# A graph layer's tensor product, built with features on partitions

## What is computed

```
def tensor_product(x_e, sh, w, C):          # C: [64, 9, 128], once for keys, once for values
    acc = sh[:, 0:1] * (x_e @ C[:, 0, :])
    for s in range(1, S):
        acc = acc + sh[:, s:s + 1] * (x_e @ C[:, s, :])
    return acc * w
```

## Time and profile before

| | |
|---|---|
| median of the runs | 3732.7 us |
| the profiled execution's own time | 3729.88 us |
| its span, first to last instruction | 3728.2 us |
| granted TensorE clock, mean | 0.942 |
| TensorE / VectorE / ScalarE / GpSimd busy | 89% / 77% / 34% / 55% |
| first edge loop, stage between, second edge loop | 170 to 1242, to 1406, to 3592 us |

### The profile page before, as it was taken

One profiled execution on the slowest core, in us unless ns is written; L12 is line 12 of the kernel. 1 busy time (PEld: TensorE's weight loads), 2 busy tenths in 40 slices (PEclk: granted clock), 3 DMA queues, 4 the chain that ended last, 5 costly groups with the idle time before them and its releaser, 6 DMA issues. The chain is left out here.

```text
span 3728.2 us, 86642 instructions
## 1 busy us (share of the span) xinstructions
PE 3330.0 (89%) x25947; PEld 3178.9 (85%) x25947; DVE 2877.5 (77%) x5292; ACT 1285.0 (34%) x3333; POOL 2055.4 (55%) x1999
## 2 busy tenths in 40 slices
PE   2099999999999337999999999999999999999963
PEld 1088888888888237999999999999999999999953
DVE  4366666666666227999999999999999999999943
ACT  1033333333333113444444444444444444444420
POOL 2577777777777435555555555555555555555540
PEclk9599999999999658999999999999999999999975
DMA  8399999999999313444444444444444444444420
GB/s 339 86 268 280 279 279 279 279 280 279 279 280 279 105 46 105 127 126 132 131 124 129 131 129 124 130 132 126 125 132 132 124 128 131 130 124 129 132 78 29
DMA packets 843789, 622.16 MB, mean 167 GB/s; under 512 B 490431, under 2 KB 732803, under 8 KB 843452
## 3 DMA queue, kind: packets, MB, share of 16 engines
q1 hardware_dynamic: 667110, 500.09, 44.2%
q0 software_dynamic: 56640, 87.65, 9.7%
q10 hardware_dynamic: 119982, 33.79, 4.1%
HBM read 335.87 MB, written 286.31 MB: 167 GB/s over the span
## 5 line engine op out<-in xcount | busy, mean ns | idle before, releaser
L1305 POOL DMA_INDIRECT xg<-h_tab,src_i x808 | 861.5, 1066 | 220.8 <-issue 127.2
L789 POOL DMA_INDIRECT kv<-kv_tab,src_i x808 | 762.1, 943 | 285.7 <-issue 188.2
L1315 POOL TENSOR_TENSOR kq<-kvs,q_of 128x512 f32<-128x512 f32 x202 | 260.6, 1290 | 837.7 <-DVE kvs L1491 837.7
L1401 ACT ACTIVATE z_hi<-bank 128x512 fp32r<-128x512 f32 x808 | 439.4, 595 | 802.9 <-PE bank L1333 802.9
L1357 PE MATMUL bank<-C_hi,z_hi 128*128 128x256 f32 x4040 | 682.2, 299 | 0.0
L1357 PE MATMUL bank<-C_lo,z_hi 128*128 128x256 f32 x4040 | 612.2, 281 | 0.0
L1481 DVE TENSOR_TENSOR z_lo<-bank,z_hi 128x512 fp32r<-128x512 f32 x808 | 520.5, 686 | 113.5 <-ACT z_hi L1401 113.4
L1357 PEld LDWEIGHTS bank<-C_hi,z_hi 128*128 128x128 f32 x4040 | 537.8, 191 | 0.3
L1357 PEld LDWEIGHTS bank<-C_lo,z_hi 128*128 128x128 f32 x4040 | 535.3, 188 | 0.0
L1357 PE MATMUL bank<-C_hi,z_lo 128*128 128x256 f32 x3232 | 516.2, 281 | 0.0
L913 DVE TENSOR_TENSOR wsb<-bank,b 128x512 f32<-128x512 f32 x404 | 279.3, 691 | 298.7 <-PE bank L977 298.3
(11 more groups left out here) (248 smaller groups left out, 4754.4 us busy)
## 6 DMA issues: line engine op xcount, KB each, us to landing
w_tab<-wsb SPq DMA_DIRECT2D x202, 512.0 KB, 3.4
win<-w_tab SPq DMA_DIRECT2D x202, 512.0 KB, 3.6
sum_edge<-rowt SPq DMA_DIRECT2D x202, 288.0 KB, 2.5
q_edge<-zq SPq DMA_DIRECT2D x202, 256.0 KB
qs<-q_edge SPq DMA_DIRECT2D x202, 256.0 KB, 2.8
sum_edge<-rows ACTq DMA_DIRECT2D x202, 136.0 KB
qs<-q_edge SPq DMA_DIRECT2D x202, 128.0 KB
drow<-dst_tab SPq DMA_DIRECT2D x202, 128.0 KB, 3.2
```

The source lines that it names most:

```text
L789: pool.indirect_dma_start(kv[b][:, q, :], None, kv0_tab, bass.IndirectOffsetOnAxis(ap=src_i[:, i * Q + q:i * Q + q + 1], axis=0))\
L1305: pool.indirect_dma_start(xg[b][:, q, :], None, h1_tab, bass.IndirectOffsetOnAxis(ap=src_i[:, i * Q + q:i * Q + q + 1], axis=0))\
L1315: pool.tensor_tensor(kq[:, :].rearrange("p (q o) -> p q o", q=Q), kvs[b][:, :, 0:O1], q_of[b % 2][:, :].rearrange("p (q o) -> p q o", q=Q) ...
L1401: nc.scalar.activation(z_hi[b % 2][:, k, :], bank[ZB[k]][:, :], ACT.Copy).then_inc(hi_out, 1)
```

## The change

z is no longer built with edges on partitions and turned. The node rows are turned instead (two transposes), ScalarE writes the turned rows `xT` twice (features on both halves of the partitions), and VectorE multiplies `xT` with spherical numbers that are already the same on all 64 partitions of a half. Of the four pairs of such rows, two are loaded repeated from DRAM (`sh`), and two are spread by TensorE into PSUM from a high and a low part (`sh_split`, eight rows, with a selection matrix `pick`); the ninth number is loaded repeated too (`sh_last`). z then lies in SBUF, and the high and low parts are formed from there, 1024 columns at a time. The comparison for `same1` goes from VectorE to ScalarE as four squares and one relu. For all this the spherical numbers must lie turned in DRAM: the stage between the loops gets a part that loads them, 101 passes at a time on 101 (or 100) partitions, rearranges them and stores three tables. The core of the diff:

```
+            SG = NST // 2
+            sh_rows = [sb(f"sh_rows{g}", [SG, ST, S], F32, ph) for g in range(2)]
+            sh_parts = sb("sh_parts", [SG, 5, ST], F32, ph)
+            sh_split = sb("sh_split", [SG, 8, ST], F32R, ph)
...
+                    def load_sh_rows(a):
+                        last_full = (NST - 1) * ST
+                        sp.dma_start(sh_rows[0][:, :, :], a[0:SG * ST, :].rearrange("(p e) s -> p e s", p=SG))\
+                          .then_inc(sh_rows_in, 16)
+                        sp.dma_start(sh_rows[1][0:NST - 1 - SG, :, :],
+                                     a[SG * ST:last_full, :].rearrange("(p e) s -> p e s", e=ST)).then_inc(sh_rows_in, 16)
+                        sp.dma_start(sh_rows[1][NST - 1 - SG:NST - SG, 0:TAIL, :], a[last_full:E, :].unsqueeze(0))\
+                          .then_inc(sh_rows_in, 16)
...
                     sp.dma_start(car[:, :, :], carry0_tab[0:N, :].rearrange("(p j) d -> p j d", j=NJ)).then_inc(car_got, 16)
+                    for g in range(2):
+                        sp.wait_ge(sh_parts_set, g + 1)
+                        sp.dma_start(sh_tab[g * SG:(g + 1) * SG], sh_parts[:, 0:4, :]).then_inc(sh_put, 16)
+                        sp.dma_start(sh_last_tab[g * SG:(g + 1) * SG, :], sh_parts[:, 4, :]).then_inc(sh_put, 16)
+                        sp.wait_ge(sh_split_set, g + 1)
+                        sp.dma_start(sh_split_tab[g * SG:(g + 1) * SG], sh_split[:, :, :].bitcast(F32)).then_inc(sh_put, 16)
                     sp.wait_ge(h1_ready, 1)
...
+                    act.wait_ge(sh_rows_in, 48)
+                    for g in range(2):
+                        if g:
+                            act.wait_ge(sh_put, 48)
+                        nc.scalar.activation(sh_split[:, 0:4, :], sh_rows[g][:, :, 4:S - 1].rearrange("p e c -> p c e"), ACT.Copy)\
+                                 .then_inc(sh_split_hi, 1)
...
+                        ins.then_inc(sh_parts_set, 1)
...
                     dve.sem_inc(shift_ready, 1)
+                    for g in range(2):
+                        dve.wait_ge(sh_split_hi, g + 1)
+                        dve.tensor_tensor(sh_split[:, 4:8, :], sh_rows[g][:, :, 4:S - 1].rearrange("p e c -> p c e"),
+                                          sh_split[:, 0:4, :].bitcast(F32), ALU.subtract).then_inc(sh_split_set, 1)
                     dve.wait_ge(own_got, 16 * NJ)
...
-                    pipelined(sp, [(load_sh, 3), (load_drow, 2), (load_q, 2), (load_mask, 1), (store, -4), (load_w, 1)], RING)
+                    pipelined(sp, [(load_split, 4), (load_sh_last, 4), (load_sh, 3), (load_drow, 2), (load_q, 2), (load_mask, 1), (store, -4), (load_w, 1)], RING)
...
-                    unrolled([(times_q, -1), (gather_x, 4)], RING)
+                    unrolled([(times_q, -1), (gather_x, 5)], RING)
...
-                    pipelined(pe, [(t_z(0), 1), (t_z(1), 1), (turn_max, -2), (sums, -3), (m_acc(0), 0), (t_z(2), 1),
-                                   (t_z(3), 1), (m_acc(1), 0), (t_z(4), 1), (spread_q, 0), (m_acc(2), 0),
-                                   (turn_logits, -1), (m_acc(3), 0)], RING)
+                    pipelined(pe, [(turn_x, 3), (turn_max, -2), (sums, -3), (m_acc(0), 0), (spread_q, 0), (m_acc(1), 0),
+                                   (turn_logits, -1), (m_acc(2), 0), (m_acc(3), 0), (spread_sh, 3)], RING)
...
-                    pipelined(act, [(hi(0), 1), (hi(1), 1), (copy_max, -2), (weights, -2), (take_sums, -3), (hi(2), 1),
-                                    (hi(3), 1), (hi(4), 1), (take_q, 0)], RING)
+                    pipelined(act, [(hi(0), 1), (copy_max, -2), (weights, -2), (take_x, 3), (take_sums, -3), (take_q, 0),
+                                    (hi(1), 1), (hi_last, 1), (apart, 1), (build, 1)], RING)
...
-                    pipelined(dve, [(product(1), -1), (lo(0), 1), (lo(1), 1), (subtract, -2), (outer(0), 2), (lo(2), 1),
-                                    (lo(3), 1), (logits, -1), (weigh, -2), (outer(1), 2), (lo(4), 1), (build, 1),
-                                    (segment_max, -1), (product(0), 0)], RING)
+                    pipelined(dve, [(product(1), -1), (subtract, -2), (outer_spread, 2), (logits, -1), (weigh, -2), (lo(0), 1),
+                                    (outer, 2), (lo(1), 1), (lo_last, 1), (outer_last, 3), (segment_max, -1),
+                                    (product(0), 0)], RING)
```

More of the change, by code:

```diff
@@ new lines, in apart @@
+                    def apart(it, i, b):
+                        act.wait_ge(drow_in[b % 2], 16 * (2 * it + b // 2 + 1))
+                        need(act, sum_mm, i - RING + 1)
+                        for q in range(Q):
+                            ins = nc.scalar.activation(same[b][:, q, :], drow[b % 2][:, q * P:(q + 1) * P], ACT.Square,
+                                                       bias=dst_e[:, bass.ds(i * Q + q, 1)], scale=-1.0)
+                        ins.then_inc(apart_ready, 1)
@@ L1409, in take_q, with build @@
+                    def build(it, i, b):
+                        act.wait_ge(apart_ready, i + 1)
+                        nc.scalar.activation(same[b][:, :, :], same[b][:, :, :], ACT.Relu, bias=one[:, :], scale=-1.0)\
+                                 .then_inc(same_ready, 1)
+                    act.wait_ge(max_zero, 4)
                     def take_q(it, i, b):
@@ new lines, in _ @@
+                    dve.memset(one[:, :], 1.0).then_inc(max_zero, 1)
+                    for c in range(2):
+                        dve.tensor_tensor(pick[c][:, :].rearrange("p (r i) -> p r i", r=2),
+                                          bcast(ident[0:8, 2 * c:2 * c + 2], 2, D), bcast(ident[0:8, 2 * c + 4:2 * c + 6], 2, D),
+                                          ALU.add).then_inc(max_zero, 1)
+                    dve.memset(seg_max[:, :], 0.0).then_inc(max_zero, 1)
+                    dve.wait_ge(max_zero, 4)
@@ new lines, in outer, with outer_spread @@
+                    def outer(it, i, b):
+                        dve.wait_ge(x_out, i + 1)
+                        dve.wait_ge(sh_in[b % 2], 32 * (2 * it + b // 2 + 1))
+                        need(dve, lo_out, i * 3 - 4)
+                        dve.tensor_tensor(z[b % 2][:, 0:2, :], bcast(xT[b % 2][:, :], 1, 2), sh[b % 2][:, :, :], ALU.mult)\
+                           .then_inc(z_ready, 1)
+                    def outer_spread(it, i, b):
+                        dve.wait_ge(x_out, i + 1)
+                        dve.wait_ge(sh_mm, i + 1)
+                        need(dve, lo_out, i * 3 - 4)
+                        for c in range(2):
+                            dve.tensor_tensor(z[b % 2][:, 2 + c, :], bank[SH_BANK + c][:, :], xT[b % 2][:, :], ALU.mult)\
+                               .then_inc(z_ready, 1)
@@ L1481, in stage, with lo_last @@
[L1481 removed]
+                            c = slice(2 * k, 2 * k + 2)
+                            dve.tensor_tensor(z_lo[b % 2][:, c, :], z[b % 2][:, c, :], z_hi[b % 2][:, c, :].bitcast(F32),
                                               ALU.subtract).then_inc(lo_out, 1)
                         return stage
+                    def lo_last(it, i, b):
+                        dve.wait_ge(hi_out, i * 3 + 3)
+                        need(dve, a_mm, i * 2 - 2)
+                        for r in range(2):
+                            f, g = rows_of[r], rows_of[1 - r]
+                            ins = dve.tensor_tensor(of_half(z_hi[b % 2][g, 4, :], r),
+                                                    z_last[b % 2][f, :].rearrange("p (h e) -> p h e", e=P),
+                                                    of_half(z_hi[b % 2][f, 4, :], r).bitcast(F32), ALU.subtract)
+                        ins.then_inc(lo_out, 1)
```

186 lines of the change are left out of this document (108 added, 78 removed).

## The result

The changed kernel takes 3722.9 us (median of nine runs, 3719.7 to 3724.84) against 3731.77 us for the kernel before on the same chip: a ratio of 0.9973, 95% interval [0.9963, 0.9984]. It is faster by 0.27%, 9 us, where 29 were forecast (3703). Its profiled execution took 3722.9 us, with a span of 3721.1. The kernel before, run again beside the experiments, had medians of 3733.4 to 3735.5, so that a difference between an experiment and the changed kernel is good to some 4 us; the ratios are each taken against the kernel before beside it. One of the four executions of experiment 8's kernel took 3879.38 us at a lower granted clock (0.912, the others 0.935 to 0.938) and is not in its ratio.

What follows compares the result with a forecast made beforehand. TensorE's issue was taken to bound the second edge loop, VectorE soon after. 3729.9 - 236 (loop) + 3 (fill) + 203 (stage between the loops) = 3700, median 3703 us; range 3640 to 3800.

Steps and rivals of the forecast that it cites:

- the gain in the loop: Second edge loop: 202 passes falling from 10.67 to 9.5 us each, 236 us gained, less 3 for the longer fill.
- TensorE in a pass: Second edge loop: 18 transposes removed, two transposes and two 512-column matmuls added; 10.67 becomes 9.43 us (9.19 to 9.91).
- upper end of 0.48 for a matmul: `spread_sh` on TensorE: a 512-column matmul takes at most 0.48 us, as two passes over 512 columns; 0.24 was taken.
- The pass: Second edge loop: 9.5 us a pass taken, as TensorE 9.43, VectorE 9.36 and ring 9.2 leave no slack for late starts.
- the fill: Second edge loop: filling three passes ahead instead of two costs 3 us.
- the 2.8 us that I added: Whole kernel: the median of the runs stands 2.8 us above the profiled execution, so 3700 becomes 3703.
- VectorE, ScalarE, ring: Second edge loop, per pass: VectorE 9.26 us, 9.36 with a wait; ScalarE 7.5; ring of waits from `take_q` round TensorE 9.2.
- The stage: Between the loops: copies over 101 partitions run on one DMA engine at 26 GB/s, so the stage costs 203 us more.
- The rival with 16 engines: Stage between the loops: 101-partition copies spread over 16 engines or nearly so; stage +25, time 3525; chance 0.15.
- the slower engine: Stage between the loops: one-engine copies overlap less or run below 26 GB/s; at 22, 52 us more, 3755; chance 0.10.
- Ring and VectorE together: Second edge loop: late `lo(1)` and scans hold up `turn_max` on TensorE; at a 10.0 us pass, 3804; chance 0.17.
- table load: ScalarE in the second edge loop: Square or Relu needs another table than Exp; pass 10.2, about 3845 us; chance 0.02.

Runs made afterwards that it cites:

- experiment 8: Kernel loading all eight rows repeated, one product in `outer_spread`'s place: that product reads one operand from PSUM; ratio 0.9759 against the kernel before.
- experiment 2: Changed kernel with the two spreading matmuls issued twice in a row, four in a pass; 3812.61 us, one run.
- Experiment 1: Changed kernel with `pick` and `sh_split` padded with zeros to 128 partitions, so spreading matmuls have 128 rows; 3680.87 us, ratio 0.9853.
- experiment 9: Changed kernel with the comparison for `same1` back on VectorE; 3800.01 us, one run.
- experiments 3 and 4: Changed kernel with other group sizes in the stage between the loops: 112 and 90 passes, 3542.85 us, ratio 0.948; 100 and 102, 3608.24 us.
- experiment 6: Changed kernel with all eight rows loaded repeated, no `spread_sh`, products beside each other, groups of 112 and 90; 3722.9 us, ratio 0.9971.
- experiment 5: Changed kernel with spreading matmuls padded to 128 rows and groups of 112 and 90 passes together; 3502.53 us, ratio 0.9382.

## Why the prediction was wrong

Direction, mechanism and the stage were right; the gain in the loop was forecast too large, and since the stage's cost eats almost all of it, the gain left is 9 us for 29.

- **TensorE in a pass: the step that failed.** I priced `spread_sh` at 0.48 us, as twice two 256-column matmuls, "since all operands have the type of that row". It took 0.86. The two matmuls do cost 0.47 (experiment 2); what I left out is the change from matmuls 128 rows high to ones of eight rows and back, 0.39 us once a pass. Experiment 1 takes the low height away and gets 0.22 us a pass and 42 us in all back. 0.17 stays: at full height spread and transposes together take 0.81, against 0.47 + 0.17 (the 0.17 is `turn_x` alone, 2506.14 to 2506.31). What that last part is, I did not settle. My upper end of 0.48 for a matmul would have covered it, but as columns, not as a pause.
- **The pass.** The error of +0.38 was hidden in part: `m_acc` takes 1.64 instead of 1.68, four times 0.04, and `turn_x` 0.17 instead of 0.21. So 9.43 becomes 9.62; the 9.5 that I took had 0.07 of it as room for late starts, of which none came. Against 9.5 the loop lost 0.12 x 202 = 24 us. With the fill at 6 us for 3 (what is left of the loop's 206) and the stage at 199 for 203 that makes the 23 us by which the profiled execution missed 3700. The median misses 3703 by 20 only because the 2.8 us that I added for it did not come: here both are 3722.9.
- **VectorE, ScalarE, ring.** 9.29 and 7.80 a pass; neither stops TensorE. The margin of VectorE was as thin as forecast: with the comparison's 0.69 us put back it is busy for 98 percent of the time and the pass is 10.0 (experiment 9).
- **The stage.** Right to 4 us, by two errors that cancel in part: copies of 101x2048 with a step of nine numbers take 3.83 us and not 1.9, and the stores still landed 3 us earlier than at 26 GB/s. That these cancel was luck; the one engine for 101 partitions, which makes up the cost, was not. The rival with 16 engines fell (share 0.07 at 31 GB/s, experiments 3 and 4), and the slower engine too. (That rival speaks of five spans of 79 + 103 + 103 us; they are three, and its 52 us are right for three.)
- **The rivals of the loop.** Ring and VectorE together would have shown TensorE stopping in each pass; it was busy for all 500 us. No table load came.

The Trainium skill (TensorEngine Tiling (Array Packing), "Key Properties") has "Mode switching requires drain", without a figure. The trace agrees if eight rows count as another mode than 128: 0.39 us for there and back. A weight tile that is narrower but 128 rows high, `turn_logits` with 32 columns, shows no such gap here (its load takes 0.10 from 2501.91, and the next one starts at 2502.01). I had not weighed that sentence.

## What to carry to other kernels

When two large terms cancel, price the small new instruction of the bound engine as it stands in the stream, with its neighbours: a matmul over few rows (eight here) between matmuls over 128 costs the change of height too, and padding the rows with zeros can be cheaper. Look at the number of partitions of every large copy before anything else: 101 and 101 instead of 112 and 90 cost 180 us here, and the repair was a choice of two numbers. Before an engine is given work to fill a wait for GpSimd, see whether both read SBUF with two operands; an operand in PSUM made the difference.

## What was not expected of the hardware

- A change between matmuls of 8 and of 128 rows: 0.20 us ahead of the first load and about 0.19 behind (experiments 1 and 2). No other height was run.
- A product on VectorE with both operands in SBUF and GpSimd's product do not run at once: `kq` takes 2298 ns beside it, 1291 with VectorE idle (experiment 6's version) and 1280 beside a product with one operand in PSUM (the changed kernel; 1291 in experiment 8, where they overlap in part). The Trainium skill (SBUF — State Buffer, "SBUF: two separate sides") calls the port pair that both use "an **exclusive lock**, not a bandwidth split"; the 1.0 us of delay agrees.
- GpSimd's gather of node rows slowed too: its mean grew from 1064 ns before to 1198 after and 1437 in experiment 5. From before to after VectorE's work with two SBUF operands grew beside it, from after to experiment 5 it did not. It may be the same exclusion; no run here separates it from other causes.
- The DMA engines were full at 250 GB/s when four rows were repeated over 64 partitions for each half (share 1.01), while the fills of the kernel before reach 422 at the same share. Why these copies move fewer bytes per busy engine was not tried.
